# Graph layer on one core: W applied after the sums over adj, LayerNorm in row layout on the vector engines, output blocks in groups of 6, 2, 6, 2

## The chip, the cores and the metric

The kernel runs on one core of a Trainium2 chip. Five engines work side by side, each on its own list of instructions, and meet only at semaphores: TensorE (PE: matrix products into the eight PSUM banks), VectorE (DVE), ScalarE (ACT), GpSimd (POOL) and SyncE (SP), which here issues every transfer. The metric is the device time of one execution in microseconds (us); lower is better. Before the change it is 763.18 us, the median of three runs (762.74 to 763.41).

## The reference

`x` is 8192 x 128, `adj` is 8192 x 8192 and nearly all of the data (268 MB), `W` is 128 x 128, `b` has 128 values; all are float32.

```python
def _layernorm(x, axis=-1, eps=1e-05):
    m = jnp.mean(x, axis=axis, keepdims=True)
    v = jnp.var(x, axis=axis, keepdims=True)
    return (x - m) / jnp.sqrt(v + eps)

h = jnp.maximum(_layernorm(x, axis=-1), 0.0)
support = jnp.matmul(h, W)
out = jnp.matmul(adj, support) + b
x = x + jax.nn.relu(out)
```

So the layer is x + relu(adj (h W) + b). Since matrix products can be regrouped, adj (h W) is also (adj h) W.

## The kernel before

The output is computed transposed: 16 blocks of 512 columns (one column for a row of the output), each block in one PSUM bank of 128 x 512. A bank gathers the sum over 64 tiles of 128 rows of `support`. The blocks are taken in groups of 6, 5 and 5 (`WIDTHS`), and a group passes once over all 64 tiles; for one tile and one group ("a step") SP brings 128 x 3072 or 128 x 2560 numbers of adj into one of four slots of `adj_tile`.

The products run in TensorE's reduced float32 form (F32R). To keep float32 accuracy each operand is split in a rounded high part and what is left, and three of the four products are added: high with high, low of the weights with high of adj, high with low. In each step, therefore:

- ACT copies the tile to `adj_high` (line 269) and the 128 x 128 tile of support to `sup_high` (line 253).
- DVE subtracts: `adj_low` (line 339) and `sup_low` (line 321).
- PE issues three products for each bank (lines 425 and 432), 18 in a step of group 0 and 15 in the others. A load of 128 x 128 weights goes with each.

`adj_high` and `adj_low` have two slots each, so ACT waits for the products of the step before last (`high_used`), DVE too (`products_done`), and SP waits until DVE is through with the step four back (`low_ready`).

Support is made during the first group, four tiles (a "round") at a time. x comes in transposed, so mean and variance lie across partitions and are taken on TensorE: `center` (line 367) multiplies a block of x by a centering matrix in plain float32, DVE rectifies it (line 292), ACT squares the centered values (line 234), `project` takes the variances (line 378, four products with one column) and rectified x times W (line 381, four products), POOL raises the variance to the power of -0.5 (line 222), and DVE scales the result into `support` (line 302). Two blocks are done ahead of the first step; the other 14 lie inside 14 rounds of group 0.

All eight banks are in use: six for group 0, one each for `center` and `support`; the later groups reuse the banks of the group before. A group's first step (`opens`) waits bank by bank until ACT has drained the old sums through relu with the bias (line 241); DVE adds x (line 311), and SP stores. The last step of all is cut into pieces, one per bank (lines 404, 266, 332), and followed by drains, adds and stores (line 200). The order of the work on each engine is that of the code, with loops over the middle rounds of each group.

Of the kernel before, what the change touches and what calls it, by code (L numbers as in the profile page):

```python
# [5 lines left out]
P = 128  # L26
BANK = 512
# [4 lines left out]
UNROLL = BANK // P  # L32
ROUNDS = TILES // UNROLL
WIDTHS = [6, 5, 5]
FIRST_BLOCK = [0, 6, 11]
ADJ_SLOTS = UNROLL
SPLIT_SLOTS = 2
WEIGHT_SLOTS = UNROLL


DRAINED = [[0, 3, 1, 2], [0, 2, 1, 2]]


STORED_LATE = range(1, FIRST_BLOCK[-1])
RELU_SLOTS = 6
CENTER_BANK, SUPPORT_BANK = 6, 7
# [3 lines left out]
ACT = mybir.ActivationFunctionType  # L50
F32 = mybir.dt.float32
# [3 lines left out]
def gnn_layer(nc, x_blocks, adj_groups, W, b, out_blocks):  # L55
    assert sum(WIDTHS) == COL_BLOCKS and ADJ_SLOTS == WEIGHT_SLOTS == UNROLL
    with ExitStack() as ctx:
# [6 lines left out]
        widest = max(WIDTHS) * BANK  # L64
        xT = sb("xT", [P, COL_BLOCKS, BANK])
        support = sb("support", [P, TILES, P])
        adj_tile = sb("adj_tile", [P, ADJ_SLOTS, widest])
        adj_high = sb("adj_high", [P, SPLIT_SLOTS, widest], F32R)
        adj_low = sb("adj_low", [P, SPLIT_SLOTS, widest], F32R)
        sup_high = sb("sup_high", [P, WEIGHT_SLOTS, P], F32R)  # L70
        sup_low = sb("sup_low", [P, WEIGHT_SLOTS, P], F32R)
        W_sb = sb("W_sb", [P, P])
        bias = sb("bias", [P, 1])
        centering = sb("centering", [P, P])
        mean_col = sb("mean_col", [P, 1])
        minus_half = sb("minus_half", [P, UNROLL])
        squares = sb("squares", [P, BANK])
        rectified = sb("rectified", [P, BANK])
        var_eps = sb("var_eps", [P, UNROLL])
        rstd = sb("rstd", [P, UNROLL])  # L80
        relu_out = sb("relu_out", [P, RELU_SLOTS, BANK])
        banks = ctx.enter_context(nc.psum_tensor("banks", [P, PSUM_BANKS, BANK], F32))
        centered_ps = banks[:, CENTER_BANK, :]
        var_ps = banks[:, CENTER_BANK, 0:UNROLL]
        support_ps = banks[:, SUPPORT_BANK, :]

        adj_landed = [sem(f"adj_landed{s}") for s in range(ADJ_SLOTS)]
        piece_landed = [sem(f"piece_landed{c}") for c in range(WIDTHS[-1])]
        piece_high = sem("piece_high")
        piece_low = sem("piece_low")  # L90
        piece_products = sem("piece_products")
        x_landed = sem("x_landed")
        params_landed = sem("params_landed")
        centering_zeroed = sem("centering_zeroed")
        constants_ready = sem("constants_ready")
        high_ready = sem("high_ready")
        low_ready = sem("low_ready")
        sup_low_ready = sem("sup_low_ready")
        high_used = sem("high_used")
        products_done = sem("products_done")  # L100
        centered = sem("centered")
        squared = sem("squared")
        rectified_ready = sem("rectified_ready")
        projected = sem("projected")
        var_ready = sem("var_ready")
        rstd_ready = sem("rstd_ready")
        support_ready = sem("support_ready")
        bank_drained = sem("bank_drained")
        output_ready = sem("output_ready")
        early_stored = sem("early_stored")  # L110
        late_stored = sem("late_stored")
        banks_stored = sem("banks_stored")
        block = ctx.enter_context(nc.Block())

        def in_all_groups(eng, round_steps):

            round_steps(0, 0, True, True)
            with eng.Fori(1, ROUNDS - 2) as k:  # L120
                round_steps(0, k, True, True)
            round_steps(0, ROUNDS - 2, True, False)
            round_steps(0, ROUNDS - 1, False, False)
            for g in range(1, len(WIDTHS)):
                round_steps(g, 0, False, False)
# [343 lines left out]
```

## Time and profile before

| what | us |
|---|---|
| median of three runs | 763.18 (762.74 to 763.41) |
| profiled execution, its own time: span from first to last instruction | 760.3 |
| difference of the median to the span | 2.9 |
| PE busy with products | 747.8 (98%) |
| DVE busy | 644.2 (85%) |
| ACT busy | 536.4 (71%) |
| POOL busy | 16.9 (2%) |
| bytes moved | 277.04 MB, 364 GB/s over the span |

The page says how long each engine was busy, but products are pipelined and their ends are modelled, so the time of a product is read from the distance between starts and not from its shown length. The page also gives the granted clock of TensorE: 1.000 over the whole execution, the upper of its two levels (2.4 GHz).

### The profile page before, as it was taken

Reading aid. Unit: us, or ns where it says so; the run is one execution under the profiler, and the core shown is the slowest. Engines: PE = TensorE matmul, PEld = TensorE weight load, DVE = VectorE, ACT = ScalarE, POOL = GpSimd, SP = SyncE. Lnnn points to the kernel's source line nnn. Section 1 sums busy time; section 2 is a strip of 40 time slices with the busy share of each in tenths; the row PEclk is TensorE's granted clock in tenths of the full one; section 3 lists DMA queues with packets and bytes.
Section 4 is the critical chain, followed back from the end, with each engine's and each line's share of the span. In section 5 each row is a group of like instructions: output and inputs, shape, how many; then the busy total and the mean of one; then the engine's idle time right before and its main releaser. Section 6 shows DMA issues by size and latency. Waiting matters only on the chain.

```text
span 760.3 us, 10345 instructions
## 1 busy us (share of the span) xinstructions
PE 747.8 (98%) x3360; PEld 615.6 (81%) x3360; DVE 644.2 (85%) x452; ACT 536.4 (71%) x421; POOL 16.9 (2%) x24
## 2 busy tenths in 40 slices
PE   6999999999999999999999999999999999999997
PEld 4888888888888888788888888888788888888886
DVE  2988888888888888898889888888999898888987
ACT  3766666666666666787777777777877777777775
POOL 0000000000000000000000000000000000000000
PEclk9999999999999999999999999999999999999999
DMA  8899898999999989989999999999999999999997
GB/s 344 350 342 356 331 363 331 335 358 338 349 352 333 357 320 337 357 336 382 391 372 380 395 385 390 375 379 404 386 362 390 394 383 383 392 387 393 367 394 300
DMA packets 32987, 277.04 MB, mean 364 GB/s; under 512 B 3664, under 2 KB 3792, under 8 KB 8528
## 3 DMA queue, kind: packets, MB, share of 16 engines
q1 hardware_dynamic: 32976, 276.90, 94.4%
q8 instruction: 6, 0.10, 0.0%
q14 instruction: 5, 0.04, 0.0%
HBM read 272.70 MB, written 4.19 MB: 364 GB/s over the span
## 4 chain that ended last, share of the span: by engine, by line
PE 97%; ACT 1%; DVE 1%; issue 1%; DMA 0%; ACTq 0%
PE banks L425 61%; PE banks L432 30%; PE banks L381 2%; PE banks L367 2%; PE banks L378 2%; DVE xT L311 0%; DMA xT<-x_blocks 0%; ACT adj_high L269 0%; ACT relu_out L241 0%; DVE rectified L292 0%; ACT squares L234 0%; PE banks L404 0%; DVE var_eps L297 0%; ACTq L261 0%; ACTq L240 0%
## 5 line engine op out<-in xcount | busy, mean ns | idle before, releaser
L339 DVE TENSOR_TENSOR adj_low<-adj_tile,adj_high 128x2560 fp32r<-128x2560 f32 (+1 forms) x191 | 573.7, 3004 | 99.9 <-ACT adj_high L269 99.0
L269 ACT ACTIVATE adj_high<-adj_tile 128x2560 fp32r<-128x2560 f32 (+1 forms) x191 | 476.0, 2492 | 197.2 <-issue 89.7
L425 PE MATMUL banks<-adj_high,sup_high 128*128 128x512 f32 x1019 | 272.9, 398 | 1.3 <-ACT relu_out L241 1.3
L425 PE MATMUL banks<-adj_high,sup_low 128*128 128x512 f32 x1019 | 264.8, 390 | 0.0
L432 PE MATMUL banks<-adj_low,sup_high 128*128 128x512 f32 x1019 | 262.2, 389 | 0.0
L425 PEld LDWEIGHTS banks<-adj_high,sup_high 128*128 128x128 f32 x1019 | 190.9, 188 | 47.7 <-issue 6.7
L425 PEld LDWEIGHTS banks<-adj_high,sup_low 128*128 128x128 f32 x1019 | 191.8, 188 | 39.6
L432 PEld LDWEIGHTS banks<-adj_low,sup_high 128*128 128x128 f32 x1019 | 191.4, 188 | 39.7
L253 ACT ACTIVATE sup_high<-support 128x128 fp32r (+1 forms) x192 | 56.1, 292 | 0.0
L321 DVE TENSOR_TENSOR sup_low<-support,sup_high 128x128 fp32r<-128x128 f32 x192 | 54.6, 285 | 0.9 <-ACT sup_high L253 0.9
L378 PEld LDWEIGHTS banks<-mean_col,squares 128*128 128x128 f32 x128 | 18.2, 208 | 7.2 <-ACT squares L234 3.1
L234 ACT ACTIVATE squares<-banks 128x512 f32<-128x512 f32 x16 | 9.6, 599 | 19.0 <-DVE rectified L292 19.0
L222 POOL TENSOR_TENSOR rstd<-var_eps,minus_half 128x4 f32<-128x4 f32 x16 | 16.1, 1008 | 272.4 <-DVE var_eps L297 272.4
L367 PE MATMUL banks<-xT,centering 128*128 (+1 forms) x32 | 18.4, 659 | 3.7 <-DMA xT<-x_blocks 3.4
L381 PE MATMUL banks<-W_sb,rectified 128*128 128x128 f32 x128 | 20.0, 305 | 0.0
L378 PE MATMUL banks<-mean_col,squares 128*128 128x1 f32 x128 | 17.0, 254 | 3.0 <-ACT squares L234 3.0
L381 PEld LDWEIGHTS banks<-W_sb,rectified 128*128 128x128 f32 x128 | 17.3, 210 | 0.0
L292 DVE TENSOR_SCALAR rectified<-banks 128x512 f32<-128x512 f32 x16 | 10.9, 683 | 5.8 <-PE banks L367 5.8
L241 ACT ACTIVATE relu_out<-banks,bias 128x512 f32<-128x512 f32 x16 | 10.3, 677 | 2.4 <-PE banks L404 2.4
L302 DVE TENSOR_TENSOR support<-banks,rstd 128x512 f32 (+1 forms) x16 | 11.0, 684 | 1.2 <-POOL rstd L222 1.2
L311 DVE TENSOR_TENSOR xT<-xT,relu_out 128x512 f32<-128x512 f32 x16 | 10.5, 687 | 0.8 <-ACT relu_out L241 0.8
L367 PEld LDWEIGHTS banks<-xT,centering 128*128 128x128 f32 x32 | 6.3, 205 | 5.1 <-issue 3.9
(18 smaller groups left out, 19.3 us busy)
## 6 DMA issues: line engine op xcount, KB each, us to landing
adj_tile<-adj SPq DMA_DIRECT2D x127, 1280.0 KB, 7.6
adj_tile<-adj SPq DMA_DIRECT2D x64, 1536.0 KB, 8.4
xT<-x_blocks SPq DMA_DIRECT2D x16, 256.0 KB, 8.3
out_blocks<-xT SPq DMA_DIRECT2D x1, 2560.0 KB, 13.4
out_blocks<-xT SPq DMA_DIRECT2D x6, 256.0 KB, 2.5
adj_tile<-adj SPq DMA_DIRECT2D x5, 256.0 KB, 5.7
W_sb<-W SPq DMA_DIRECT2D x1, 64.0 KB, 2.1
bias<-b SPq DMA_DIRECT2D x1, 0.5 KB, 3.1
```

Source lines behind the costliest of these rows:

```text
L222: nc.gpsimd.tensor_tensor(rstd[:, :], var_eps[:, :], minus_half[:, :], ALU.pow)\
L253: nc.scalar.activation(sup_high[:, r:r + 1, :], support[:, bass.ds(k * UNROLL + r, 1), :], ACT.Copy).then_inc(high_ready, 1)
L269: nc.scalar.activation(adj_high[:, r % SPLIT_SLOTS, 0:width], adj_tile[:, r, 0:width], ACT.Copy).then_inc(high_ready, 1)
L292: nc.vector.tensor_scalar(rectified[:, :], centered_ps, 0.0, None, ALU.max)\
L302: nc.vector.tensor_tensor(support[:, bass.ds(n * UNROLL, UNROLL), :], support_ps.rearrange("p (t d) -> p t d", d=P), rstd[:, :].rearrange( ...
L321: nc.vector.tensor_tensor(sup_low[:, r:r + 1, :], support[:, bass.ds(k * UNROLL + r, 1), :], sup_high[:, r:r + 1, :].bitcast(F32), ALU.sub ...
L339: nc.vector.tensor_tensor(adj_low[:, r % SPLIT_SLOTS, 0:width], adj_tile[:, r, 0:width], adj_high[:, r % SPLIT_SLOTS, 0:width].bitcast(F32 ...
L367: nc.tensor.matmul(banks[:, CENTER_BANK:CENTER_BANK + 1, :], centering[:, :], xT[:, bass.ds(n, 1), :], start=True, stop=True).then_inc(cen ...
L378: nc.tensor.matmul(var_ps[:, i:i + 1], squares[:, i * P:(i + 1) * P], mean_col[:, :], start=True, stop=True)
L381: last = nc.tensor.matmul(support_ps[:, i * P:(i + 1) * P], rectified[:, i * P:(i + 1) * P], W_sb[:, :], start=True, stop=True)
L425: last = nc.tensor.matmul(banks[:, n % PSUM_BANKS, :], sup[:, r, :], adj[:, r % SPLIT_SLOTS, c * BANK:(c + 1) * BANK], start=opens and i = ...
L432: last = nc.tensor.matmul(banks[:, (FIRST_BLOCK[g] + c) % PSUM_BANKS, :], sup[:, r, :], adj[:, r % SPLIT_SLOTS, c * BANK:(c + 1) * BANK], ...
```

## The change

1. **Order of the products.** The sums over tiles are now taken of h itself, not of h W. When a bank holds its finished 128 x 512 sum, ACT copies it out rounded (`sum_high`), DVE takes the rest (`sum_low`), and PE multiplies both by W (split in `W_high` and `W_low`) in three products back into the same bank (`project`). Relu with bias and the addition of x follow.
2. **LayerNorm in row layout.** A second copy of x in rows (`x_rows`) is loaded during group 0. Mean and variance now lie along the free axis: DVE sums (`tensor_reduce`) and scales to the negative mean, ACT squares with that bias and an accumulated sum, DVE makes variance plus eps, POOL raises to -0.5 and normalizes four tiles of 128 x 128 (`z_sb`), ACT rectifies and rounds to `h_high`, DVE makes `h_low` with one `scalar_tensor_tensor`. TensorE has no part in it.
3. **Halves kept.** `h_high` and `h_low` hold all 64 tiles, so no step after group 0 splits weights again. x itself no longer stays on the chip: its blocks are loaded a second time, transposed, when a block is finished (`load_residual`).
4. **Groups.** 6, 2, 6, 2 blocks. Groups of two take two tiles per step (`DEPTHS`), so a step moves 128 x 2048 numbers and has 12 products. Groups of six use banks 0 to 5, groups of two banks 6 and 7, so a group is drained while the next one runs, one block every four steps from step 3 on.
5. **Buffers and edges.** The high part has three slots instead of two. The first tile of adj comes in four pieces (1, 1, 2, 2 blocks) with one tile of x ahead; the last step comes in two pieces. All steps are written out, without loops.

The core of the diff:

```diff
-WIDTHS = [6, 5, 5]
-FIRST_BLOCK = [0, 6, 11]
...
+WIDTHS = [6, 2, 6, 2]
+DEPTHS = [1, 2, 1, 2]
+FIRST_BLOCK = [0, 6, 8, 14]
+FIRST_BANK = [0, 6, 0, 6]
+STEPS = [TILES // d for d in DEPTHS]
+FIRST_STEP = [sum(STEPS[:g]) for g in range(len(WIDTHS))]
+ALL_STEPS = sum(STEPS)
+LAST = ALL_STEPS - 1
...
+OPENING = [1, 1, 2, 2]
+BATCHES = [(0, 1), (1, 4)] + [(t, t + 4) for t in range(4, TILES, 4)]
+X_SLOTS = 4
+Z_SLOTS = 2
+DRAIN_AT, DRAIN_EVERY = 3, 4
+PROJECT_AFTER, RELU_AFTER, STORE_AFTER = 1, 5, 10
+OUT_SLOTS = 2
...
+            def load_residual(n):
+                if n < X_SLOTS:
+                    sp.wait_ge(z_ready, TILES)
+                else:
+                    sp.wait_ge(stored[n % X_SLOTS], 16 * (n // X_SLOTS))
+                sp.dma_start(x_sb[:, n % X_SLOTS, :], x_blocks[n]).then_inc(res_landed[n % X_SLOTS], 16)
...
+            for j, (first, end) in enumerate(BATCHES):
+                pool.wait_ge(var_ready, j + 1)
+                nc.gpsimd.tensor_tensor(rstd[:, first:end], var_eps[:, first:end],
+                                        minus_half[:, first:end], ALU.pow).then_inc(rstd_ready, 1)
+                pool.wait_ge(rstd_ready, j + 1)
+                if j >= 3:
+                    pool.wait_ge(h_low_ready, BATCHES[j - Z_SLOTS][1])
+                for t in range(first, end):
+                    cols = slice(t % 4 * P, t % 4 * P + P)
+                    nc.gpsimd.tensor_scalar(z_sb[:, x_slot(j) % Z_SLOTS, cols],
+                                            x_sb[:, x_slot(j), cols],
+                                            neg_mean[:, t:t + 1], rstd[:, t:t + 1],
+                                            ALU.add, ALU.mult).then_inc(z_ready, 1)
...
+            def square(j, tiles):
+                act.wait_ge(mean_ready, j + 1)
+                for t in tiles:
+                    cols = slice(t % 4 * P, t % 4 * P + P)
+                    if t >= 4:
+                        act.wait_ge(squared, t - 3)
+                    nc.scalar.activation(squares[:, t % 4, :], x_sb[:, x_slot(j), cols], ACT.Square,
+                                         bias=neg_mean[:, t:t + 1],
...
+            def rectify(j):
+                first, end = BATCHES[j]
+                act.wait_ge(z_ready, end)
+                at = first % 4
+                nc.scalar.activation(h_high[:, first:end, :],
+                                     z_sb[:, x_slot(j) % Z_SLOTS, at * P:(at + end - first) * P]
+                                     .rearrange("p (t d) -> p t d", d=P),
+                                     ACT.Relu).then_inc(h_high_ready, 1)
...
+            def sum_to_high(n):
+                if n >= OUT_SLOTS:
+                    act.wait_ge(projected, n - OUT_SLOTS + 1)
+                nc.scalar.activation(sum_high[:, n % OUT_SLOTS, :], banks[:, bank_of(n), :],
+                                     ACT.Copy).then_inc(sum_high_ready, 1)
...
+                if t >= HIGH_SLOTS:
+                    act.wait_ge(low_ready, t - HIGH_SLOTS + 1)
+                    act.wait_ge(high_used, t - HIGH_SLOTS + 1)
...
+                j = (t - 1) // 4 + 2
+                if g == 0 and j < len(BATCHES):
+                    first = BATCHES[j][0]
+                    if t % 4 == 1:
+                        square(j, range(first, first + 2))
+                    if t % 4 == 2:
+                        square(j, range(first + 2, first + 4))
+                    if t % 4 == 0:
...
+            def mean(j):
+                first, end = BATCHES[j]
+                at = first % 4
+                if j == 0:
+                    dve.wait_ge(x_first_landed, 16)
+                else:
+                    dve.wait_ge(x_landed[x_slot(j)], x_landed_count(j))
+                nc.vector.tensor_reduce(neg_sum[:, first:end],
+                                        x_sb[:, x_slot(j), at * P:(at + end - first) * P]
+                                        .rearrange("p (t d) -> p t d", d=P),
+                                        AXIS.X, ALU.add, negate=True).then_inc(summed, 1)
+                dve.wait_ge(summed, j + 1)
+                nc.vector.tensor_scalar(neg_mean[:, first:end], neg_sum[:, first:end], 1.0 / P, None,
...
+            def rectified_low(j):
+                first, end = BATCHES[j]
+                at = first % 4
+                dve.wait_ge(h_high_ready, j + 1)
+                nc.vector.scalar_tensor_tensor(h_low[:, first:end, :],
+                                               z_sb[:, x_slot(j) % Z_SLOTS, at * P:(at + end - first) * P]
+                                               .rearrange("p (t d) -> p t d", d=P),
+                                               0.0, h_high[:, first:end, :].bitcast(F32),
+                                               ALU.max, ALU.subtract).then_inc(h_low_ready, end - first)
...
+            def sum_to_low(n):
+                dve.wait_ge(sum_high_ready, n + 1)
+                nc.vector.tensor_tensor(sum_low[:, n % OUT_SLOTS, :], banks[:, bank_of(n), :],
+                                        sum_high[:, n % OUT_SLOTS, :].bitcast(F32),
+                                        ALU.subtract).then_inc(sum_low_ready, 1)
...
+                if t >= LOW_SLOTS:
+                    dve.wait_ge(products_done, t - LOW_SLOTS + 1)
...
+                    if t % 4 == 2:
+                        variance(j)
+                    if t % 4 == 0:
+                        rectified_low(j)
+                        if j + 1 < len(BATCHES):
+                            mean(j + 1)
...
+            def product(t, c, k, h, tile, slot, start=False, stop=False):
+                g = group_of(t)
+                at = (c * DEPTHS[g] + k) * BANK
+                return nc.tensor.matmul(banks[:, FIRST_BANK[g] + c, :],
+                                        h[:, (t - FIRST_STEP[g]) * DEPTHS[g] + k, :],
+                                        tile[:, slot, at:at + BANK], start=start, stop=stop)
...
+                pe.wait_ge(sum_low_ready, n + 1)
+                nc.tensor.matmul(out, W_high[:, :], sum_high[:, slot, :], start=True, stop=False)
+                nc.tensor.matmul(out, W_low[:, :], sum_high[:, slot, :], start=False, stop=False)
+                nc.tensor.matmul(out, W_high[:, :], sum_low[:, slot, :], start=False, stop=True) \
+                  .then_inc(projected, 1)
...
+                if opens and g >= 2:
+                    pe.wait_ge(relu_ready, FIRST_BLOCK[g - 1])
+                for c, k in order:
+                    product(t, c, k, h_high, high, t % HIGH_SLOTS, start=opens and k == 0)
+                h_is_there(t, h_low_ready, True)
+                for c, k in order:
+                    last = product(t, c, k, h_low, high, t % HIGH_SLOTS)
+                last.then_inc(high_used, 1)
+                pe.wait_ge(low_ready, t + 1)
+                for c, k in order:
+                    last = product(t, c, k, h_high, low, t % LOW_SLOTS, stop=closes and k == DEPTHS[g] - 1)
+                last.then_inc(products_done, 1)
+                n = drained_at(t, PROJECT_AFTER)
+                if n is not None:
+                    project(n)
```

How the instructions stand on TensorE inside the first group, before the change (`xT`, `centering`, `squares`, `rectified` belong to the LayerNorm; the rest are the steps' products):

```order
L432 MATMUL banks<-adj_low,sup_high 128x512 x6
L367 MATMUL banks<-xT,centering 128x512
L425 MATMUL banks<-adj_high,sup_high 128x512 x6
L425 MATMUL banks<-adj_high,sup_low 128x512 x6
...
L378 MATMUL banks<-mean_col,squares 128x1 x4
L381 MATMUL banks<-W_sb,rectified 128x128 x4
```

After the change, at the seam of groups 0 and 1 and at the first block that is projected (four steps into group 1):

```order
L444 MATMUL banks<-low,h_high 128x512 x6
L444 MATMUL banks<-high,h_high 128x512 x4
L444 MATMUL banks<-high,h_low 128x512 x4
L444 MATMUL banks<-low,h_high 128x512 x4
...
L462 MATMUL banks<-sum_high,W_high 128x512
L463 MATMUL banks<-sum_high,W_low 128x512
L464 MATMUL banks<-sum_low,W_high 128x512
```

Nothing but the steps' products is left inside group 0, and three more products stand behind a step for each finished block. The same seam before, where one bank after the other is opened:

```order
L432 MATMUL banks<-adj_low,sup_high 128x512 x6
L425 MATMUL banks<-adj_high,sup_high 128x512
L425 MATMUL banks<-adj_high,sup_low 128x512
...
L432 MATMUL banks<-adj_low,sup_high 128x512 x5
L425 MATMUL banks<-adj_high,sup_high 128x512 x5
```

The seam's single products, each pair behind a wait for a drained bank, are gone: the next group opens in banks that nothing else holds. VectorE in group 0 before, from the variance of one round on (`sup_low` is the split of the weights):

```order
L297 TENSOR_SCALAR var_eps<-banks 128x4
L321 TENSOR_TENSOR sup_low<-support,sup_high 128x128
L339 TENSOR_TENSOR adj_low<-adj_tile,adj_high 128x3072
L302 TENSOR_TENSOR support<-banks,rstd 128x512
L292 TENSOR_SCALAR rectified<-banks 128x512
```

and after, over four steps:

```order
L353 TENSOR_SCALAR var_eps<-sum_squares 128x4
L416 TENSOR_TENSOR low<-raw,high 128x3072 x2
L360 SCALAR_TENSOR_TENSOR h_low<-z_sb,h_high 128x512
L342 TENSOR_REDUCE neg_sum<-x_sb 128x4
L347 TENSOR_SCALAR neg_mean<-neg_sum 128x4
L416 TENSOR_TENSOR low<-raw,high 128x3072 x2
```

The per-step split of weights went out, and the sum over rows came in. Two big subtractions now stand between the variance and the instruction that needs what POOL and ACT make of it (`h_low`). GpSimd after the change, from its first power on (batches of one, three and then four tiles):

```order
L227 TENSOR_TENSOR rstd<-var_eps,minus_half 128x1
L235 TENSOR_SCALAR z_sb<-x_sb,neg_mean,rstd 128x128
L227 TENSOR_TENSOR rstd<-var_eps,minus_half 128x3
L235 TENSOR_SCALAR z_sb<-x_sb,neg_mean,rstd 128x128 x3
L227 TENSOR_TENSOR rstd<-var_eps,minus_half 128x4
L235 TENSOR_SCALAR z_sb<-x_sb,neg_mean,rstd 128x128 x4
```

Before, it had only the power (L222) in each round; the normalizing of tiles moved to it from DVE's L302.

## Rows read from the trace of the kernel before

**Rows 1.** the page: engines (busy us, share, instructions), DMA totals, the chain that ended last

```profile
PE 747.8 (98%) x3360; PEld 615.6 (81%) x3360; DVE 644.2 (85%) x452; ACT 536.4 (71%) x421; POOL 16.9 (2%) x24
...
DMA packets 32987, 277.04 MB, mean 364 GB/s; under 512 B 3664, under 2 KB 3792, under 8 KB 8528
...
PE 97%; ACT 1%; DVE 1%; issue 1%; DMA 0%; ACTq 0%
```

**Rows 2.** timeline of PE and others in one round: start, us, engine, line, operation

```profile
61.36 1.52 PE L425 MATMUL banks<-adj_high,sup_high 128*128 128x512 f32 x6
...
62.72 1.52 PE L425 MATMUL banks<-adj_high,sup_low 128*128 128x512 f32 x6
...
65.44 1.02 PE L367 MATMUL banks<-xT,centering 128*128 x2
...
75.30 1.14 PE L381 MATMUL banks<-W_sb,rectified 128*128 128x128 f32 x8
...
80.38 1.52 PE L425 MATMUL banks<-adj_high,sup_high 128*128 128x512 f32 x6
```

**Rows 3.** timeline of the opening

```profile
3.35 2.04 PE L367 MATMUL banks<-xT,centering 128*128 128x512 f32 x2 [3.35 <-DMA xT<-x_blocks]
...
23.32 1.52 PE L425 MATMUL banks<-adj_high,sup_high 128*128 128x512 f32 x6
```

**Rows 4.** timeline at the seam of groups 0 and 1

```profile
318.16 0.39 PE L425 MATMUL banks<-adj_high,sup_high 128*128 128x512 f32 x1
...
320.01 0.50 PE L425 MATMUL banks<-adj_high,sup_high 128*128 128x512 f32 x1 [0.79 <-ACT relu_out L241]
...
322.89 1.31 PE L425 MATMUL banks<-adj_high,sup_high 128*128 128x512 f32 x5
```

**Rows 5.** instructions by shape: busy us, mean ns of one, idle before

```profile
L339 DVE TENSOR_TENSOR adj_low<-adj_tile,adj_high 128x2560 fp32r<-128x2560 f32 x127 | 358.8, 2825 | 44.4 <-ACT adj_high L269 43.5
...
L339 DVE TENSOR_TENSOR adj_low<-adj_tile,adj_high 128x3072 fp32r<-128x3072 f32 x64 | 214.9, 3357 | 55.5 <-ACT adj_high L269 55.5
...
L269 ACT ACTIVATE adj_high<-adj_tile 128x3072 fp32r<-128x3072 f32 x64 | 177.6, 2774 | 91.2 <-issue 78.0 <-PE banks L425 13.2
...
L253 ACT ACTIVATE sup_high<-support 128x128 fp32r x164 | 47.9, 292 | 0.0
...
L292 DVE TENSOR_SCALAR rectified<-banks 128x512 f32<-128x512 f32 x16 | 10.9, 683 | 5.8 <-PE banks L367 5.8
...
L241 ACT ACTIVATE relu_out<-banks,bias 128x512 f32<-128x512 f32 x16 | 10.3, 677 | 2.4 <-PE banks L404 2.4
...
L297 DVE TENSOR_SCALAR var_eps<-banks 128x4 f32<-128x4 f32 x16 | 2.5, 155 | 4.6 <-PE banks L381 4.6
...
L211 POOL TENSOR_SCALAR_AFFINE_SELECT centering<-centering 128x128 f32<-128x128 f32 x1 | 0.3, 292 | 0.2 <-issue 0.2
```

**Rows 6.** stretches: length, busy of each engine, granted clock, DMA share, GB/s

```profile
4.00:20.00 16.00, 12.68 (x41) 9.08 (x40) 5.18 (x6) 6.73 (x6) 1.02 (x1) 1.00 0.99 405
...
340.00:510.00 170.00, 170.00 (x752) 140.86 (x751) 151.28 (x101) 127.20 (x101) 0.00 (x0) 1.00 0.98 384
516.00:536.00 20.00, 20.00 (x90) 16.55 (x89) 17.83 (x13) 15.13 (x12) 0.00 (x0) 1.00 1.00 406
```

**Rows 7.** timeline of GpSimd's power beside VectorE

```profile
11.00 1.02 POOL L222 TENSOR_TENSOR rstd<-var_eps,minus_half 128x4 f32<-128x4 f32 x1 [9.52 <-DVE var_eps L297]
...
24.17 0.28 DVE L321 TENSOR_TENSOR sup_low<-support,sup_high 128x128 fp32r<-128x128 f32 x1
24.33 1.01 POOL L222 TENSOR_TENSOR rstd<-var_eps,minus_half 128x4 f32<-128x4 f32 x1 [12.31 <-DVE var_eps L297]
...
25.09 3.36 DVE L339 TENSOR_TENSOR adj_low<-adj_tile,adj_high 128x3072 fp32r<-128x3072 f32 x1 [0.64 <-ACT adj_high L269]
```

**Rows 8.** timeline of the end

```profile
753.88 3.41 DVE L311 TENSOR_TENSOR xT<-xT,relu_out 128x512 f32<-128x512 f32 x5 [0.80 <-ACT relu_out L241]
...
755.45 0.39 PE L404 MATMUL banks<-adj_low,sup_high 128*128 128x512 f32 x1
```

More of the change, by code:

```diff
@@ L130, in step_of, with columns @@
[L130 to L150 removed]
+        def columns(t):
+            g = group_of(t)
+            return WIDTHS[g] * DEPTHS[g] * BANK
@@ L216, in inverse_deviation @@
[L216 to L227 removed]
+            pool.wait_ge(constants_ready, 1)
@@ new lines, in add_x @@
+            def add_x(n):
+                dve.wait_ge(relu_ready, n + 1)
+                dve.wait_ge(res_landed[n % X_SLOTS], 16 * (n // X_SLOTS + 1))
+                nc.vector.tensor_tensor(x_sb[:, n % X_SLOTS, :], x_sb[:, n % X_SLOTS, :],
+                                        relu_out[:, n % OUT_SLOTS, :], ALU.add).then_inc(output_ready, 1)
+            mean(0)
+            variance(0)
+            rectified_low(0)
+            opening(0)
+            mean(1)
+            opening(1)
+            variance(1)
@@ L359, in _ @@
+            for c in range(WIDTHS[-1]):
+                sum_to_low(FIRST_BLOCK[-1] + c)
+            for c in range(WIDTHS[-1]):
+                add_x(FIRST_BLOCK[-1] + c)
         @block.tensor
         def _(pe):
[L361 to L368 removed]
@@ new lines, in _ @@
+            h_is_there(0, h_high_ready, False)
+            for i in range(len(OPENING)):
+                pe.wait_ge(opening_high, i + 1)
+                if i == 0:
+                    pe.wait_ge(h_low_ready, 1)
+                for c in range(sum(OPENING[:i]), sum(OPENING[:i + 1])):
+                    product(0, c, 0, h_high, high, 0, start=True)
+                    last = product(0, c, 0, h_low, high, 0)
+            last.then_inc(high_used, 1)
+            for i in range(len(OPENING)):
+                if i < len(OPENING) - 1:
+                    pe.wait_ge(opening_low, i + 1)
+                else:
+                    pe.wait_ge(low_ready, 1)
+                for c in range(sum(OPENING[:i]), sum(OPENING[:i + 1])):
+                    last = product(0, c, 0, h_high, low, 0)
@@ new lines, in _ @@
+            t = LAST
+            g = group_of(t)
+            for c in range(WIDTHS[g]):
+                pe.wait_ge(closing_high, c + 1)
+                for k in range(DEPTHS[g]):
+                    product(t, c, k, h_high, high, t % HIGH_SLOTS)
+                    product(t, c, k, h_low, high, t % HIGH_SLOTS)
+                pe.wait_ge(closing_low, c + 1)
+                for k in range(DEPTHS[g]):
+                    last = product(t, c, k, h_high, low, t % LOW_SLOTS, stop=k == DEPTHS[g] - 1)
+                last.then_inc(closing_products, 1)
@@ L448 @@
+            for c in range(WIDTHS[g]):
+                project(FIRST_BLOCK[g] + c)
 def kernel(x, adj, L0_gnn_W, L0_gnn_b):
```

539 lines of the change are left out of this document (237 added, 302 removed).

## Prediction

> **What bounds the kernel now.** I read the page first: PE is busy 98% and the chain that ended last is PE for 97% [rows 1]. No wait on that chain is worth chasing; what counts is how many products PE issues and how far apart. The timeline of one round comes next: six products take 62.72 - 61.36 = 1.36 us, so a 512-column product with its weights costs 0.2267 us [rows 2]. The granted clock is 1.00 in every stretch read, the upper level [rows 6]. The round has 72 products of adj, 72 x 0.2267 = 16.32 us, but lasts 80.38 - 61.36 = 19.02 us: the rest is `center` and `project` [rows 2]. Then the stretches: outside group 0 the DMA engines are busy 98% at 384 GB/s while PE never idles [rows 6]. So PE is the bound, DMA is close behind, and shortening PE's work is worth something only until the transfers take over. All 3072 products of adj stay: 696.4 us that nothing here removes.
>
> **The change part by part**, against the profiled span of 760.3 us.
>
> (a) LayerNorm and W leave PE in group 0: 14 rounds x (19.02 - 16.32) = **-37.8 us**. It is all on the path.
>
> (b) The opening. Before, PE first worked at 3.35, and the first step after the opening one began at 23.32 [rows 3]. After, that step (step 1) needs its tile and ACT's 2.77 us copy of it [rows 5]. Ahead of it and including it SP asks for 4.0 MB (the first tile, x, W, the tile). At 405 GB/s, the rate of 4 to 20 us [rows 6], with the queue filled by 4 us and about 0.5 MB there by then, it lands near 13. ACT's own list says the same: square, rectify, four opening pieces, and a wait for POOL's power and three normalizations put it at about 13.4. Step 1 thus begins near 16.3: -7.0. Bounds: 14 and 21. VectorE comes out of the opening late (W split, mean, opening pieces), and its first `h_low` of a full batch is about 1 us late for PE: +1.0. Together **-6.0 us**.
>
> (c) Seams. Before, opening step 64 took 322.89 - 318.16 = 4.73 us for 15 products that need 3.40 [rows 4], 1.3 too many; at the second seam PE's wait is shorter, I take 1.0. After, the new group opens in other banks: **-2.3 us**. What could be late instead is the wait for `relu_ready` at groups 2 and 3, but the last relu it needs stands at step 28 of 32 and at step 12 of 64, so it is over by then.
>
> (d) Projection: 16 blocks x 3 products, 14 of them between steps: 42 x 0.2267 = **+9.5 us**, all on PE. They wait for `sum_low`, which DVE makes a step earlier; PE stands behind it if DVE is late, so DVE's room matters (f).
>
> (e) The end. Before, 760.3 - 755.45 = 4.85 us follow the last product's start: drain, relu, add, store [rows 8]. After, a copy (about 0.65, as L241 [rows 5]), a subtraction (0.68, as L292), three products and two or three handovers come between, about 2.5 us more; the other block's share lies beside it: **+2.5 us**. Bounds +1.9 and +4.
>
> (f) ACT, DVE and POOL. In a 16.32 us round of group 0 DVE now has 4 x 3.36 = 13.4, the mean (512 elements: 0.68 as L292), `h_low` (0.68), and two small ones of 0.155 [rows 5]: 15.1 us, 93%. ACT has 4 x 2.77 + 4 x 0.29 + 0.65 = 12.9. With two slots DVE starts step t's subtraction when PE starts step t-1, so it is done 0.6 us before PE begins t, and is wanted 2.72 us into t: a batch's extra 0.9 us between is absorbed. ACT stands at `square` until DVE has the mean, over 3 us, but its third slot leaves it a whole step. In groups 1 and 3 a subtraction of 2048 columns is 3.36 - 2 x 0.53 = 2.29 (0.53 is what 512 columns add [rows 5]); with 1.37 for a draining block that is 10.5 us in four steps of 11.56. I take **0**. Bounds: -0, since PE never idles in the rounds now; above, the mean at twice its cost would fill DVE to 97%, still no wait, and ends at +15 us if each of 15 batches loses 1 us.
>
> POOL's new work: the power takes 1.01 [rows 7]; a normalization of 128 x 128 is not in the trace. Bounds 0.29 (the 128 x 128 select) and 1.01 (the power) [rows 5, 7]; I take 0.4, the nearer one in shape. From DVE's variance, at about the start of PE's step 4m+2 (m counts the rounds), power, four normalizations and rectify need 1.0 + 1.6 + 0.65, with handovers 3.7; they have 2 x 4.08 us before PE wants `h_high`. Even at 1.01 each it is 6.1 us. Cost 0, hidden by two steps of products, unless POOL is held up: that is a rival.
>
> (g) Transfers. x is read twice and stores are spread: 277.0 [rows 1] + 4.2 = 281.2 MB. Group 0 wants 104.9 MB in PE's 261.2 us, 402 GB/s. While six blocks drain, groups 1 and 3 want 4.19 MB of adj and 0.52 MB of x and output in 11.56 us, 408 GB/s. The trace held 405 and 406 where the DMA share was 0.99 and 1.00 [rows 6]. So they just keep up, with small lags: **+2 us**. Bounds: 0, and the rate of 384, shown without a loss, as a ceiling (second rival). Written-out code also brings more instruction fetches; I take them inside these 2.
>
> Sum: -37.8 - 6.0 - 2.3 + 9.5 + 2.5 + 2.0 = -32.1, a span of 728.2 us. The median of before stands 2.9 us over its span, so I forecast **731 us**. Cross-check from the front: 16.3 + 1, then 3054 + 42 products to the last, 701.9, then 7.3 after its start, makes 726.5 without transfers' lag; the same number.
>
> **Rivals.** First, POOL is held up by DVE. Each instruction of POOL would stand until the subtraction in progress ends. Variance is followed on DVE at once by the subtraction of step 4m+3 (3.36 us), so the power starts only after it, 3.6 us late; the normalizations stand behind the next subtraction, and end after it; then rectify. Counting from PE's start of step 4m+2: power 3.6 to 4.6, subtraction to 8.0, four normalizations to 9.6, rectify to 10.3, where PE wanted it at 8.2: a stall of 2.2 us in each of 15 batches, 33 us: 764. With 1.01 for a normalization it is 4.6 us, 69 in all: 800. **This is the slower case**: it decides from 0.4 us a normalization on. In the trace, L321, which reads two tiles in SBUF, ran until 24.45; the power started at 24.33 within it and took 1.01, against 1.02 on an idle DVE; and L339 started at 25.09 while the power ran until 25.34 and took its usual 3.36 [rows 5, 7]. Both speak against a lock, weakly: the overlaps are 0.12 and 0.25 us, and a power reads only four elements per partition.
>
> The Trainium skill has this very rule ("SBUF — State Buffer", Who interferes with whom): a VectorE instruction with two SBUF inputs contends with a GpSimd instruction that reads SBUF, and the later one blocks fully until the first ends. By that rule the case above would hold; the trace does not show it, and shows no long overlap either.
>
> Second, DMA becomes the bound: 384 GB/s is a ceiling and the 405 were bursts. Group 0 then takes 104.9 / 0.384 = 273 instead of 261, groups 1 and 3 36.7 / 0.384 = 95.6 instead of 91.1 each, group 2 265 instead of 262.6: +23 in place of the 2 above, **752 us**. For it: DMA share 0.98 at 384 over 170 us. Against: PE did not idle there, and demand was just that 384 to 386, so the trace does not show a ceiling; 16 and 20 us at 405 are long for a burst.
>
> The Trainium skill ("HBM Reference", Specifications) puts the bandwidth of a core that streams alone at about 425 GB/s. By that the second rival would be out and the lag of (g) near 0, 729; this case's trace reached 406 over 20 us [rows 6], and nothing in it shows 425.
>
> Third, PE loses more at the places where it newly waits, for `h_low` in each batch (f): 15 x 1 us, 746.
>
> **How the numbers follow.** Forecast 0.58 (its own range 725 to 738), third rival 0.08, DMA 0.15, POOL held up 0.19, of which more than half above 765. Of this last 0.06 is still faster, 0.02 level, 0.11 slower. That the change doesn't do what it says I rule out: in PE's list nothing but adj's products is left in group 0. A measurement of this kernel tells about 0.2%, 1.5 us. Faster 0.87, same 0.02, slower 0.11. The range from 724 (opening at 14, no lag) to 761 takes in the DMA case and the near end of the POOL case, and leaves out some 0.17.
>
> **What would show it.** (a) Starts of PE's steps in group 0 are 4.08 us apart; if 4.6 on the mean, it is a rival. (b) First full step near 16. (c) No gap on PE at the seams. (d) 48 products of W at 0.23. (f) POOL's normalizations of 0.3 to 0.5 us; if they are 3 us long or start only between DVE's subtractions, and ACT's rectify waits for POOL, the first rival holds. (g) ACT waiting for the landing of `raw` in most steps, with DMA share 1.0 at under 400 GB/s, shows the second. The forecast is wrong if the span is over 745 with DMA below 0.98 and POOL idle in the waits.

## The result and the profile after

The changed kernel takes 773.25 us (four runs, 771.54 to 775.09) against 763.26 us for the kernel before on the same chip (762.74 to 763.41): ratio over the single runs 1.0137, 95% interval 1.0117 to 1.0156 (the two medians give 1.0131). It is slower by 1.4%: a small loss, but clear of the noise, where a gain of 4% was forecast (731 us, range 724 to 761). The profiled execution has a span of 773.3 us.

Lines of the profile's page that answer to [rows 1] (the last two: busy us, mean ns | idle before, and what ended that idle time):

```profile
PE 733.7 (95%) x3120; PEld 595.4 (77%) x3120; DVE 619.8 (80%) x297; ACT 526.0 (68%) x375; POOL 129.4 (17%) x86
HBM read 276.89 MB, written 4.19 MB: 364 GB/s over the span
PE 51%; issue 19%; POOL 16%; DMA 7%; DVE 3%; ACT 2%; SPq 1%; POOLq 0%; ACTq 0%; DVEq 0%
...
L256 ACT ACTIVATE h_high<-z_sb 128x512 fp32r<-128x512 f32 (+2 forms) x17 | 10.3, 604 | 90.7 <-POOL z_sb L235 90.6
L227 POOL TENSOR_TENSOR rstd<-var_eps,minus_half 128x4 f32<-128x4 f32 (+2 forms) x17 | 38.4, 2260 | 166.5 <-DVE var_eps L353 166.5
```

PE was 97% of the chain before; now POOL has 16% of it, though it is busy for only 17% of the span. So POOL is on the chain because its results come late, not because it has much to do. Its instructions (number, min/median/max ns) are usually short and sometimes several times as long:

```profile
L235 POOL TENSOR_SCALAR z_sb<-x_sb,neg_mean,rstd x64: 440/443/3667, 4.7 to 297.7; 128x128 f32<-128x128 f32 x64
...
L227 POOL TENSOR_TENSOR rstd<-var_eps,minus_half x17: 567/1007/4140, 4.0 to 290.0; 128x4 f32<-128x4 f32 x15, 128x1 f32<-128x1 f32 x1, 128x3 f32<-128x3 f32 x1
```

The timeline of group 0 (as [rows 2]; start, us) shows where. A batch is the LayerNorm of four tiles, made once in four steps. One batch:

```profile
101.69 0.16 DVE L353 TENSOR_SCALAR var_eps<-sum_squares 128x4 f32<-128x4 f32 x1
...
101.86 6.63 DVE L416 TENSOR_TENSOR low<-raw,high 128x3072 fp32r<-128x3072 f32 x2
101.94 4.14 POOL L227 TENSOR_TENSOR rstd<-var_eps,minus_half 128x4 f32<-128x4 f32 x1 [10.38 <-DVE var_eps L353]
...
106.18 3.90 POOL L235 TENSOR_SCALAR z_sb<-x_sb,neg_mean,rstd 128x128 f32<-128x128 f32 x4
...
110.12 0.63 ACT L256 ACTIVATE h_high<-z_sb 128x512 fp32r<-128x512 f32 x1 [5.70 <-POOL z_sb L235]
...
110.89 1.77 PE L444 MATMUL banks<-high,h_high 128*128 128x512 f32 x6 [1.93 <-ACT h_high L256]
...
112.46 2.76 PE L444 MATMUL banks<-high,h_low 128*128 128x512 f32 x6
115.02 1.83 PE L444 MATMUL banks<-low,h_high 128*128 128x512 f32 x6
```

The power starts 0.08 us after a VectorE subtraction (3.36 us) and takes 4.14 us: that subtraction is over at 105.2, and the power ends 0.87 us later. The first normalization starts at 106.18, within the second subtraction, which is over at 108.49, and ends at 108.80 after 2.62 us; the other three then take 0.44 us each. An instruction that takes so much longer beside a subtraction is called held from here on. ACT and PE stand behind. The next batch is of another kind:

```profile
120.46 1.01 POOL L227 TENSOR_TENSOR rstd<-var_eps,minus_half 128x4 f32<-128x4 f32 x1 [10.37 <-DVE var_eps L353]
...
120.97 3.36 DVE L416 TENSOR_TENSOR low<-raw,high 128x3072 fp32r<-128x3072 f32 x1 [0.60 <-PE banks L444]
121.57 7.59 POOL L235 TENSOR_SCALAR z_sb<-x_sb,neg_mean,rstd 128x128 f32<-128x128 f32 x4
...
125.05 3.36 DVE L416 TENSOR_TENSOR low<-raw,high 128x3072 fp32r<-128x3072 f32 x1 [0.72 <-PE banks L444]
...
129.97 1.39 PE L444 MATMUL banks<-high,h_high 128*128 128x512 f32 x5 [0.87 <-ACT h_high L256]
```

Here PE's own lateness has left a gap of 0.60 us on VectorE before the subtraction at 120.97. The power starts in it and takes its free 1.01 us; two of the four normalizations are held instead (3.08 and 3.67 us), and PE waits 0.87 us. The two kinds alternate. Between the opening and the end of the kernel the granted clock falls only at the long waits, for the steps behind them (stretches of the same trace: length, busy of PE, PEld, DVE, ACT and POOL, clock, DMA share, GB/s):

```profile
107.00:111.00 4.00, 2.08 (x10) 1.45 (x9) 1.63 (x2) 0.88 (x2) 3.09 (x4) 1.00 0.91 323
...
112.50:114.50 2.00, 2.00 (x6) 1.62 (x5) 0.99 (x1) 2.00 (x6) 0.00 (x0) 0.50 0.95 406
115.40:120.00 4.60, 4.60 (x21) 3.79 (x20) 4.53 (x2) 4.60 (x6) 0.00 (x0) 0.98 0.73 260
```

0.50 is the lower level, 1.2 GHz: the six products from 112.46 to 115.02 are 0.427 us apart, where the upper level, 2.4 GHz, gives 0.227.

The account of group 0, steps 1 to 63, is made from the starts of PE's products: what a step lasts beyond 0.2267 us for each of its products is lost. The total is 42.0 us. Waits for `h_high` cost 3.43 + 7 x 2.09 + 7 x 1.03 = 25.3 us of it; the steps behind the long waits, at the lower level, 2.97 + 7 x 1.72 = 15.0; step 1 another 0.8; the remaining 0.9 is spread over the other steps. Groups 1, 2 and 3 lose 1.5, 1.4 and 2.2.

At the seam of groups 1 and 2 (timeline) ACT waits for a tile, and PE for ACT:

```profile
406.71 2.77 ACT L308 ACTIVATE high<-raw 128x3072 fp32r<-128x3072 f32 x1 [1.77 <-DMA raw<-adj]
...
409.54 1.66 PE L444 MATMUL banks<-high,h_high 128*128 128x512 f32 x6 [0.68 <-ACT high L308]
```

### The profile page after: what moved, and what is told of

It reads as the page before. It is cut to its first block, busy times and chain, and to the rows that moved or that the text cites. A ratio compares the mean times of both kernels' runs of the same rounds, so it can differ in the third digit from the quotient of the medians.

```text
span 773.3 us, 7777 instructions
## 1 busy us (share of the span) xinstructions
PE 733.7 (95%) x3120; PEld 595.4 (77%) x3120; DVE 619.8 (80%) x297; ACT 526.0 (68%) x375; POOL 129.4 (17%) x86
## 4 chain that ended last, share of the span: by engine, by line
PE 51%; issue 19%; POOL 16%; DMA 7%; DVE 3%; ACT 2%; SPq 1%; POOLq 0%; ACTq 0%; DVEq 0%
PE banks L444 50%; POOL z_sb L235 11%; DMA raw<-adj 7%; POOL rstd L227 5%; DVE low L416 3%; ACT high L308 2%; PE banks L462 0%; POOLq L72 0%; PE banks L464 0%; PE banks L463 0%; SPq L160 0%; SPq L179 0%; DVE sum_low L377 0%; ACT relu_out L279 0%; DVE x_sb L384 0%
## 5 line engine op out<-in xcount | busy, mean ns | idle before, releaser
L416 DVE TENSOR_TENSOR low<-raw,high 128x3072 fp32r<-128x3072 f32 (+1 forms) x190 | 570.1, 3004 | 110.0 <-PE banks L444 68.5
L308 ACT ACTIVATE high<-raw 128x3072 fp32r<-128x3072 f32 (+1 forms) x190 | 471.1, 2488 | 143.8 <-DMA raw<-adj 118.4
L444 PE MATMUL banks<-high,h_high 128*128 128x512 f32 x1024 | 272.0, 397 | 33.9 <-ACT h_high L256 22.8
L444 PE MATMUL banks<-high,h_low 128*128 128x512 f32 x1024 | 276.1, 402 | 0.0
L444 PE MATMUL banks<-low,h_high 128*128 128x512 f32 x1024 | 266.8, 393 | 1.2 <-DVE low L416 1.1
L444 PEld LDWEIGHTS banks<-high,h_high 128*128 128x128 f32 x1024 | 192.6, 189 | 82.2 <-issue 28.7
L444 PEld LDWEIGHTS banks<-high,h_low 128*128 128x128 f32 x1024 | 199.6, 195 | 42.9
L444 PEld LDWEIGHTS banks<-low,h_high 128*128 128x128 f32 x1024 | 194.6, 191 | 45.1 <-DVE low L416 3.9
L235 POOL TENSOR_SCALAR z_sb<-x_sb,neg_mean,rstd 128x128 f32<-128x128 f32 x64 | 90.6, 1426 | 1.8
L227 POOL TENSOR_TENSOR rstd<-var_eps,minus_half 128x4 f32<-128x4 f32 (+2 forms) x17 | 38.4, 2260 | 166.5 <-DVE var_eps L353 166.5
```

The costliest lines, as they stand in the source:

```text
L227: nc.gpsimd.tensor_tensor(rstd[:, first:end], var_eps[:, first:end], minus_half[:, first:end], ALU.pow).then_inc(rstd_ready, 1)
L235: nc.gpsimd.tensor_scalar(z_sb[:, x_slot(j) % Z_SLOTS, cols], x_sb[:, x_slot(j), cols], neg_mean[:, t:t + 1], rstd[:, t:t + 1], ALU.add, A ...
L308: nc.scalar.activation(high[:, t % HIGH_SLOTS, 0:columns(t)], raw[:, t % RAW_SLOTS, 0:columns(t)], ACT.Copy).then_inc(high_ready, 1)
L416: nc.vector.tensor_tensor(low[:, t % LOW_SLOTS, 0:columns(t)], raw[:, t % RAW_SLOTS, 0:columns(t)], high[:, t % HIGH_SLOTS, 0:columns(t)]. ...
L444: return nc.tensor.matmul(banks[:, FIRST_BANK[g] + c, :], h[:, (t - FIRST_STEP[g]) * DEPTHS[g] + k, :], tile[:, slot, at:at + BANK], start ...
```

## The experiments

The first six change the new kernel; 7 and 8 change the kernel of experiment 3, called version 3. "Excess" is the loss of PE in group 0 counted as above (42.0 us in the new kernel), in the profiled run.

**1. POOL writes but doesn't read.** Its normalizations become a fill with a constant, so LayerNorm's values are left out.

```diff
-nc.gpsimd.tensor_scalar(z_sb[...], x_sb[...], neg_mean[:, t:t + 1], rstd[:, t:t + 1], ALU.add, ALU.mult)
+nc.gpsimd.memset(z_sb[...], 0.5)
```

> GpSimd fills z_sb with a constant (memset) instead of normalizing, so it writes the same tiles but reads nothing from SBUF; the normalization itself is left out. Power unchanged. Theory L (a VectorE subtraction with two SBUF inputs keeps GpSimd's reads waiting until it ends): only the power can still be held, at most 3.4 us; the fills take about 0.2 us each whatever VectorE does, h_high is ready before PE wants it, PE's waits for it vanish and with them the low clock: profiled span about 731 (773.3 less the 42 us of group 0). Rival M (VectorE keeps any GpSimd instruction waiting, or GpSimd is slow for its own reasons): fills are stretched to 3 us as the normalizations are, span about 770. Rival O (the order on ACT and VectorE alone makes h late): span about 770 with fills of 0.2 us.

Measured: 736.13 us (one run), span 734.3, excess 1.8. The fill and 20 to 300 us:

```profile
L235 POOL MEMSET z_sb<- x64: 205/207/212, 4.7 to 253.9; 128x128 f32 x64
```

```profile
20.00:300.00 280.00, 278.96 (x1229) 230.27 (x1228) 251.75 (x134) 221.00 (x207) 27.90 (x75) 1.00 0.99 398
```

Sixty-four writes take 205 to 212 ns whatever VectorE does. All of the loss but 1.8 us goes with POOL's reading instructions. (The powers still read, but only one of those in the 15 full batches is held here.) The fill is also a shorter instruction than the normalization; experiment 5 keeps the normalization. The second fence settles the DMA rival as well: 398 GB/s with a share of 0.99 while PE is busy 278.96 of 280 us, so 384 was no ceiling.

**2. VectorE's subtraction in two pieces** of 1536 columns in group 0, to give POOL a handover in the middle.

```diff
+for i in range(2 if g == 0 else 1):
+    last = nc.vector.tensor_tensor(low[..., cols], raw[..., cols], high[..., cols], ALU.subtract)
```

> Each subtraction of group 0 is made in two instructions of 1536 columns (1.76 us each) instead of one of 3072 (3.36). Theory L, with waiting for the whole instruction: the longest normalization falls from 3.67 us to about 2.0 and the longest power from 4.14 to about 2.6, GpSimd gets a turn twice as often, and the waits of PE for h_high (22.8 us in all) fall by half or more: span 740 to 760. Rival B (the two engines share bandwidth, nobody waits for an end): the durations of the normalizations stay as they are in sum, span 773 to 780, since VectorE has 64 more fixed costs of about 0.1 us.

Measured: 774.52 us (one run), excess 40.3: no gain, a miss. VectorE, then POOL, in one batch:

```profile
100.44 6.76 DVE L420 TENSOR_TENSOR low<-raw,high 128x1536 fp32r<-128x1536 f32 x4
...
100.59 2.47 POOL L227 TENSOR_TENSOR rstd<-var_eps,minus_half 128x4 f32<-128x4 f32 x1 [10.45 <-DVE var_eps L353]
103.17 5.49 POOL L235 TENSOR_SCALAR z_sb<-x_sb,neg_mean,rstd 128x128 f32<-128x128 f32 x4
```

The power is indeed held for one piece only, 2.47 us instead of 4.14. But the normalization that starts at 103.17 gets in at neither of the next two handovers (about 103.8 and 105.5); it ends at 107.36, just after VectorE's row of pieces does (107.2). The longest takes 4.20 us. The two held normalizations of the next batch pass over a boundary too. So a boundary between two subtractions that follow each other at once is no opening to count on. Why the power got in at one and the normalization at none stays open.

**3. ACT normalizes**, with scale and bias; only the power stays on POOL, and VectorE makes the bias from mean and power.

```diff
+dve.wait_ge(rstd_ready, j + 1)        # at t % 4 == 3
+nc.vector.tensor_tensor(shift[...], neg_mean[...], rstd[...], ALU.mult)
-nc.gpsimd.tensor_scalar(z_sb[...], x_sb[...], ..., ALU.add, ALU.mult)
+nc.scalar.activation(z_sb[...], x_sb[...], ACT.Identity, bias=shift[:, t:t + 1], scale=rstd[:, t:t + 1])
```

> The four normalizations of a batch go from GpSimd to ACT (Identity with scale and bias per row; the bias column neg_mean*rstd is one 128x4 product on VectorE after the subtraction of step 4m+3); only the power stays on GpSimd. Theory L: the power can be held once for 3.4 us, and VectorE then waits up to 1.2 us for it, PE loses 0 to 0.8 us a batch and keeps its clock: 731 to 746. If the power's wait alone were enough for the stalls: 765 or more. If ACT with about 1.2 us more per round becomes late: PE waits for ACT high, 745 to 760.

Measured: 737.85 us (735.99 to 741.18), ratio to the kernel before 0.9682 (0.9654 to 0.9711), excess 3.2.

```profile
107.64 3.36 DVE L424 TENSOR_TENSOR low<-raw,high 128x3072 fp32r<-128x3072 f32 x1
...
107.73 4.14 POOL L229 TENSOR_TENSOR rstd<-var_eps,minus_half 128x4 f32<-128x4 f32 x1 [12.27 <-DVE var_eps L353]
...
111.90 0.16 DVE L359 TENSOR_TENSOR shift<-neg_mean,rstd 128x4 f32<-128x4 f32 x1 [0.90 <-POOL rstd L229]
```

The power is held more often than before (in 12 of the 15 full batches), and PE hardly waits: one held instruction fits into two steps, and two, one behind the other, don't. This version is faster than both kernels.

**4. LayerNorm a round earlier** (squares, mean, variance, power and normalizations of batch j + 1 instead of j; rectify stays).

```diff
-        square(j, range(first, first + 2))
+        square(j + 1, range(first, first + 2))
-        variance(j)
+        variance(j + 1)
```

> Mean, squares, variance, power and normalization of a batch are made four steps earlier than in the changed kernel; rectify and h_low stay where they are. Nothing is taken from any engine. Theory L with latency as the harm: powers and normalizations are held as long as before (durations up to 4.1 and 3.7 us), but end in time; PE's waits for h_high go to about 0, the clock stays up, and the time falls by 40 us to 733 (729 to 738), faster than both kernels. Rival V (VectorE is also held by GpSimd or is simply full): PE waits for low or h_low instead, 745 to 765. Rival O (order on ACT and VectorE): no change, 773.

Measured: 741.09 us (738.29 to 742.19), ratio 0.9708 (0.9687 to 0.9729), excess 1.8. The normalizations:

```profile
L236 POOL TENSOR_SCALAR z_sb<-x_sb,neg_mean,rstd x64: 438/448/4190, 4.5 to 246.4; 128x128 f32<-128x128 f32 x64
```

They are held even longer (the profile's page has a mean of 1907 ns, against 1426 in the new kernel), and PE doesn't wait for `h_high` in any batch. A held POOL costs nothing by itself: what costs is `h_high` being late. The time is 8 us over the 733 that was expected, 3 over the top of its range. Step 1 starts 2.2 us later after the first product than in the new kernel (14.2 against 12.0, for the extra batch before it), and group 3 lost 5.6 us.

**5. The second operand of group 0's subtraction from PSUM.** Two zeroed banks stand in for `high`, so `low` is a copy of adj there: part of the computation is left out, the instruction stays as long.

```diff
-nc.vector.tensor_tensor(low[...], raw[...], high[...], ALU.subtract)
+nc.vector.tensor_tensor(low[...], raw[...], banks[:, 6:8, :]..., ALU.subtract)   # g == 0
```

> The changed kernel, but in group 0 VectorE's subtraction takes its second operand from two idle PSUM banks (zeroed once) instead of from the high part in SBUF: same output, same size, one SBUF input instead of two; the low parts of group 0 are therefore not the true ones. GpSimd's work is unchanged and reads SBUF. Theory L (it is the second SBUF input that keeps GpSimd waiting): every normalization takes 0.44 us and every power 1.0 whatever VectorE does, PE's waits for h_high vanish, span 731 to 736. Rival M (any VectorE instruction that reads the same memory, or SBUF traffic as such, slows GpSimd): normalizations are stretched to 3 us as before and the span stays near 773.

Measured: 738.37 us (one run), excess 1.8.

```profile
105.82 1.01 POOL L228 TENSOR_TENSOR rstd<-var_eps,minus_half 128x4 f32<-128x4 f32 x1 [13.46 <-DVE var_eps L354]
...
106.09 3.35 DVE L420 TENSOR_TENSOR low<-raw,banks 128x3072 fp32r<-128x3072 f32 x1 [0.36 <-PE banks L456]
...
106.93 1.75 POOL L236 TENSOR_SCALAR z_sb<-x_sb,neg_mean,rstd 128x128 f32<-128x128 f32 x4
```

All four normalizations run inside the subtraction, at 0.45 us each. The subtraction takes 3.35 us, as it did, and writes as much. Only where its second input comes from has changed, and the loss is gone. The one normalization that is still long (1.52 us) stands in the opening, beside a subtraction that still has both inputs in SBUF.

**6. Normalization with two constants** in place of the mean and the power per row: POOL then reads one operand, and z isn't the normalized x.

```diff
-neg_mean[:, t:t + 1], rstd[:, t:t + 1], ALU.add, ALU.mult
+0.25, 1.5, ALU.add, ALU.mult
```

> GpSimd's normalization takes two constants instead of the columns neg_mean and rstd, so it reads one SBUF operand instead of three; the true mean and deviation are left out of h. In e2 the first normalization of a batch stood through two handovers between back-to-back subtractions. Theory S (each SBUF operand needs its own turn at the port): with one operand it gets in at the first handover, the longest normalization is at most 3.4 us also where two subtractions follow each other, and PE's waits for h_high fall from 22.8 to under 15 us, span 750 to 765. Rival T (it is the instruction that waits, whatever it reads): durations and span as before, 4 us and 773.

Measured: 758.88 us (one run), excess 25.4; PE waits for `h_high` 19.6 us, more than expected.

```profile
L235 POOL TENSOR_SCALAR z_sb<-x_sb x64: 289/292/3503, 4.6 to 282.5; 128x128 f32<-128x128 f32 x64
```

```profile
60.00:300.00 240.00, 223.37 (x971) 181.06 (x971) 198.87 (x105) 170.71 (x165) 96.07 (x65) 1.00 0.93 361
```

One operand is enough to be held. What shortens a batch is mainly the free length, 0.29 instead of 0.44 us, four times. A batch costs 1.42 to 1.47 us here, 14 times (and 1.89 once), and the clock stays up in all of them. So 15 waits alone cost about 22 us, and the new kernel's 15 us at the lower level are a term of their own. None of the batches is short, either: the power is held in 14 of 15. Long and short batches alternate only in the two traces in which the clock falls (the new kernel's and experiment 2's); that the slow steps are what opens VectorE's gap for the next power fits this, but isn't shown. Whether each operand of a held instruction needs a turn of its own isn't settled by this.

**7. Two slots for the high part instead of three**, in version 3.

```diff
-RAW_SLOTS, HIGH_SLOTS, LOW_SLOTS = 4, 3, 2
+RAW_SLOTS, HIGH_SLOTS, LOW_SLOTS = 4, 2, 2
```

> e3 (ACT normalizes) with two slots for the high part instead of three, to see what the third slot of the change is worth once GpSimd is out of the way. If my step (f) was right that ACT stands at the squares until VectorE has the mean, over 3 us, then with two slots ACT's copy comes late for PE once a round: 15 x 1 to 2 us and perhaps the low clock, span 750 to 770. If the slot was not needed: 735 to 738.

Measured: 746.32 us (one run), excess 8.7 against 3.2: at most batches PE loses about 0.5 us at a step's second or third set of products (waits of the trace):

```profile
PE banks L454 <- DVE h_low L366: 7.3, 8, 6.2
...
PE banks L454 <- DVE low L424: 2.5, 8, 0.5
```

The third slot is worth some 5.5 us in group 0 (8.5 over the whole, within which groups 1 to 3 vary by several us from run to run). The time lies between the two that were expected: the slot is needed, but for less.

**8. Residuals of groups 2 and 3 loaded earlier**, within group 2, in version 3.

```diff
+early = {FIRST_STEP[2] + 20 + 6 * i: n for i, n in enumerate((8, 9, 10, 11, 14, 15))}
+if t in early:
+    load_residual(early[t])
```

> e3, and the blocks of x that are added to output blocks 8 to 11, 14 and 15 are loaded during group 2 (where adj asks for 385 GB/s) instead of during group 3 (where adj, x and output together ask for 408); 14 and 15 go into the two tiles of z_sb. Theory D (the 1 to 6 us that PE loses in group 3 are lateness of the adj tiles behind other transfers): excess of group 3 falls under 0.5 us, time 735 (733 to 737) against 737.9 of e3. Rival E (group 3's losses are something else): same time as e3 within 1 us. The loss at the seam of groups 1 and 2, where tiles of 1.5 MB must be fetched while PE still runs steps of 2.72 us, is not touched and stays at 2 to 3 us.

Measured: 737.54 us (736.33 to 739.32), ratio 0.9662 (0.9648 to 0.9675): the same as version 3 within the intervals. Group 3 of its profiled run lost 3.9 us, where under 0.5 was expected. Four of the six loads of x that stood in group 3 were gone from it; so these loads are not what makes group 3 wait. Two loads and the stores were left in place.

## Why the prediction was wrong

**The failed step is (f)**, "Cost 0, hidden by two steps of products, unless POOL is held up". It let POOL's power and normalizations run at their free length beside VectorE's subtractions, and they don't. Group 0 lost 42.0 us, against 1.8 where POOL only writes: some 40 us where 0 stood. The first rival, given 0.19, was the case, and the sign named for it came: normalizations of up to 3.67 us, and ACT's rectify waiting for POOL. Its mechanism held almost to the number: it put a batch's stall at 2.2 us; the long batches cost 2.09. Two things in it were off, and they partly cancel. Seven of the 15 batches cost only 1.03, because a gap on VectorE lets the power through: 25.3 us where 33 were put (the first long batch, at step 3, cost 3.43). And it had no term for the clock: 15.0 us. Together 40.3. So the rival's total of 764 came within 9 us of the measured 773 in part by luck.

What shows the cause: the loss goes when POOL doesn't read (1), when VectorE's second input isn't in SBUF (5), when only one of POOL's two pieces stays (3), and when it has a round more (4). It doesn't go when the subtraction is cut in two (2), nor wholly when POOL reads less (6).

**How [rows 7] were misread.** They were taken to speak "against a lock, weakly". The first overlap was the last 0.12 us of L321. A held power ends 0.87 us after the subtraction that held it (105.21 to 106.08), 0.14 less than its free 1.01, so a wait of 0.12 would not have shown in its length. In the second the power came first, by 0.76 us. The new trace has the same pair, 120.46 and 120.97, next to one in the other order (101.86 and 101.94) that takes 4.14. An overlap in which the subtraction came second says nothing of the one in which it came first. Of that order the trace of before has only the 0.12 us beside L321, in each round, so it was no evidence against the rival, which should have had the larger chance.

That rule of the Trainium skill ("SBUF — State Buffer", Who interferes with whom) agrees with experiments 1 and 5: a VectorE instruction with two SBUF inputs blocks POOL's reads and not its writes (738.37 us with the second input in PSUM and 736.13 with POOL writing only, against 773.25). In experiment 2 POOL was held longer than the rule has it: not until the VectorE instruction that came first was over, but over two such ends, 4.20 us beside pieces of 1.75. There the measurement decides.

**(a)** Right where `h_high` isn't late: in versions 1, 3 and 5 group 0's steps are on the mean within 0.06 us of 4.08 (excess of 1.8 to 3.2 over 63 steps).

**(b)** Step 1 began at 17.91, not 16.3: 1.6 us more, inside the bounds. ACT's copy, put at 13.4, waited for the tile until 15.09:

```profile
15.09 2.77 ACT L308 ACTIVATE high<-raw 128x3072 fp32r<-128x3072 f32 x1 [1.53 <-DMA raw<-adj]
```

The 1.0 us for a late `h_low` shows where POOL isn't in the way: in experiment 1 step 4 lost 0.99 us. It is part of the 1.8 above.

**(c)** Seam of groups 0 and 1: right, products follow one another from 316.97 on (opening of group 1) with no wait. The seam of groups 1 and 2 holds a term that the prediction left out. While PE still runs steps of 2.72 us, tiles of 1.5 MB instead of 1.0 come in, so ACT waits for DMA and PE for ACT, 0.68 us in the fence above. Groups 1 and 2 together lost 2.8 us here, nearly all of it in the last two steps before this seam (1.1) and the first three from it on (1.2), and 2 to 6 in the other versions.

**(d), (e)** Right in size. All 48 products with W are there, each shown with 0.4 us as adj's are, and none of them but the last block's waits. From the start of adj's last product to the end of the span it was 6.8 us where 7.3 were put.

**(g)** 2 us put, 5.0 measured in groups 1 to 3, seams with them. The DMA rival (0.15) is out by experiment 1. The third rival, PE waiting for `h_low` in each batch, doesn't appear: PE waits for `h_low` once, in the opening, and 1.1 us for `low` in all.

**In (f)**, ACT's squares were put at 0.29 us each; they take 0.39, and each has a second instruction of 0.19 behind it. No wait of PE in group 0 beyond step 4 comes from it.

Corrected, the forecast's own sum closes: 17.9 (opening) + 42.0 (group 0) + 701.9 (products) + 5.0 (groups 1 to 3) + 6.5 (behind the last product of adj) = 773.3, for a span of 773.3. Version 3, in which the excess of group 0 is 3.2, takes 737.85, against 731.

What stays open: the 1 to 6 us that group 3 loses from one run to the next, and the order in which a held POOL is let in (2).

## What to carry to other kernels

Before work goes to GpSimd, look for VectorE instructions with two SBUF inputs, and count how many of GpSimd's reading instructions in a row must be through before their result is wanted: each one can be held to the end of a VectorE instruction or of a whole row of them. Cure it by lead (a round ahead) or by fewer links (ACT does the second); an operand in PSUM removed the hold too, here only with a stand-in for the true data. Cutting VectorE's instruction in two didn't help. Price a repeated wait of TensorE with its clock: here 15 us of the 40 were not waits.

## What was not expected of the hardware

- A wait of PE of 1.93 us was followed by a stretch at 0.50 of the clock that cost another 1.7 us, seven times out of seven; the seven waits of about 0.9 us, and experiment 6's 15 waits for `h_high` of up to 1.7 us, were not.
- GpSimd alone: power of 128 x 4 1.01 us, normalization of 128 x 128 0.44 with two row constants from SBUF, 0.29 with constants in the instruction, a fill 0.21. Held, a power took up to 4.20 us and a normalization up to 4.20 (experiments 4 and 2).
- In the other order VectorE hardly waited: two subtractions that began 0.19 us after a free normalization took 3.46 and 3.45 us instead of 3.36 (experiment 4), and those that began 0.5 us after a power took 3.36.
- Each square with an accumulated sum on ACT carries a second instruction of 187 ns to read the sum: 64 of them, 12.0 us, half of what the squares themselves take.
